# Gate and up products ahead of a data-dependent branch, in place of short products

## The chip, the cores and the metric

The kernel runs on one core of a Trainium2 chip. The metric is the device time of one execution in microseconds (us). TensorE (PE in the profile) multiplies, ScalarE (ACT), VectorE (DVE) and GpSimd (POOL) do the element work, SyncE (SP) issues the DMAs. PEld is TensorE's weight load, which overlaps its products.

## The reference

Four sequences of 1024 tokens, width 256, go through a half feed-forward step, an attention step with 16 heads, and a second half feed-forward step:

```python
x = x + 0.5 * ffn(_layernorm(x), gate_w, up_w, down_w, gate_s, up_s, down_s)
x = x + attn(_layernorm(x), Wq, Wk, Wv, Wo)          # causal, rotary, 16 heads of 16
x = x + 0.5 * ffn(_layernorm(x), gate_w, up_w, down_w, gate_s, up_s, down_s)

def ffn(xf, ...):
    g = jnp.einsum('th,ih->ti', xf, gate_w) * gate_s   # 704 hidden columns, weights -1, 0, 1
    u = jnp.einsum('th,ih->ti', xf, up_w) * up_s
    return jnp.einsum('ti,hi->th', jax.nn.silu(g) * u, down_w) * down_s
```

## The kernel before

Tokens go in chunks `c` of 512 (eight of them). The first feed-forward step works on one chunk at a time. DVE takes mean and variance of the rows (`dve_bn`, `dve_va`), POOL makes scale and shift of them (`pool_rs`, tile ROW, lines 1407 to 1412), ACT writes the normalized rows (`act_xn`, tile XN, line 1159, four operations a chunk), PE transposes them (`pe_xT`, line 996, eight products a chunk), and ACT and DVE split the result into a rounded part XH (`act_xh`, line 1165) and a rest XL (`dve_xl`, line 1267). [...]

A gate or up tile (`pe_g`, `pe_u`, line 1010) is one bank of PSUM, 128 hidden columns by 512 tokens. It takes four products of 128x512: XH and XL of the lower 128 inputs, then XH and XL of the upper 128. ACT takes silu of a gate tile (`act_silu`, tile G, line 1180), DVE multiplies it with the up tile (`dve_h`, tile HF, line 1301), ACT rounds that (`act_hh`, tile HH, line 1191), and POOL takes the rest (`pool_hl`, tile HL, line 1422, some 1.3 us each). There are two buffers of G and HF, so `dve_h` of a column block waits for `pool_hl` of the block two before it. The down projection (`pe_dn`, line 1039) reads HH and HL.

A planner (`timetable`) fixes the order on every engine before the program is built. Each engine runs its own list strictly in that order. The first PE entries are: short products on the identity IDT (`pe_warm`, line 988), the transposes of chunk 0, more short products, `pe_flag` (line 1017), one short product, `pe_branch`, then the tiles g0, g1, u0, u1, g2, u2, g3 of chunk 0, the transposes of chunk 1, the tiles g4, u3, u4, u5 of chunk 0 and g0, u0 of chunk 1, and the first half of the transposes of chunk 2. Gate tile i is written g(i), up tile i is u(i).

[...] DVE looks at the weights as they arrive (`dve_flag`, line 1273), `pe_flag` adds up over the partitions, DVE makes an integer of it (`dve_flagint`, lines 1280 and 1282, tile FLAG), and PE loads it into a register (line 1664) and branches (line 1666) into one of two copies of the rest of the program: float32r, or plain float32 where the flag is set. With the inputs of the reference the first copy runs. Between `pe_flag` and the register load stand eight short products of 128x128 in plain float32 (line 1661, `BEFORE_BRANCH = 8`), each run by the chip as two. PE goes into the branch with them queued.

The weights of gate and up come by DMA into RG and go from there by a second DMA into WG (`dma_wc0` to `dma_wc3`, line 1531). g0, g1 and u0 read columns of `dma_wc0`, u1 reads `dma_wc1`.

Of the kernel before, what the change touches and what calls it, by code (L numbers as in the profile page):

```python
# [17 lines left out]
P = 128  # L18
# [5 lines left out]
NI = 6  # L24
# [16 lines left out]
def gu_part(col):  # L41
    return next(i for i, (a, z) in enumerate(GU_COLS) if a <= col < z)
# [82 lines left out]
def e_skip(c2, j):  # L125
    return max(j - 4 * c2, 0) * P
# [202 lines left out]
BY_TANH = (0,)  # L329
AHEAD = 3.988  # L330
DOWN_FIRST = 4
BEFORE_BRANCH = 8
WARM_SPAN, WARM_SHARE, WARM_COLD = 2700.0, 0.5, 10000.0
BUSY = {"full": 0.92, "half": 0.85, "mask": 0.75, "col": 0.95}
FILL = {"full": "full", "half": "half", "mask": "half", "col": "half"}
# [86 lines left out]
def x_ring(who):  # L422
    return "X" + who
# [329 lines left out]
def macaron(nc, x_in, wgu, wd, wqkv, wo, gsc, usc, dsc, ident_in, cos_in, sin_in, mask_in, out):  # L753
    ctx = ExitStack()
    with ctx:
        cursor = [16512]

        def place(name, shape, dt=F32, at=None):
            size = int(np.prod(shape[1:])) * (2 if dt == BF16 else 4)
            off = cursor[0] if at is None else at  # L760
            t = nc.alloc_sbuf_tensor_at(name, list(shape), dt, offset=off)
            assert off + size <= 229344, (name, off + size)
            if at is None:
                cursor[0] = (off + size + 31) // 32 * 32
            return t

        def lay(at, *items):

            made = []
            for name, shape, dt in items:  # L770
                made.append(place(name, shape, dt, at=at))
                at += (int(np.prod(shape[1:])) * (2 if dt == BF16 else 4) + 31) // 32 * 32
            return made, at
# [4 lines left out]
        IDT = place("IDT", [P, P])  # L778
# [25 lines left out]
        XH = [place("XH0", [P, 2, 512], F32R)]  # L804
        XL = [place("XL0", [P, 2, 512], F32R)]
# [19 lines left out]
        OP, _ = lay(oc_at, *((f"{n}{i}", [P, 512], F32R) for i in range(4) for n in ("OL", "OH")))  # L825
# [40 lines left out]
        def f32(ap):  # L866
            return ap.bitcast(F32)
# [8 lines left out]
        def gu_slab(ph, kt, col):  # L876

            a, z = GU_COLS[gu_part(col)]
            at = 2 * a + kt * (z - a) + col - a
            return WG[ph][:, at:at + P]  # L880

        plan = timetable()
        slot, prior, emptied = plan.slot, plan.prior, plan.emptied
# [9 lines left out]
        pe, act, dve, pool, sp = (Engine(n, sems, done) for n in ("PE", "ACT", "DVE", "POOL", "SP"))  # L893
        S = sems | {signal: sems[sem] for signal, sem in EMPTIES.items() if sem in sems}

        def bank(*use):
            return psum[:, plan.bank[use][0], :]
# [5 lines left out]
        def x_slot(who, c):  # L903
            return {"a": (0,), "f1": (1, 2), "f2": (3, 0)}[who][slot[x_ring(who), (who, c)]]
# [37 lines left out]
        def wait_x_in(e, who, c, kt):  # L942
            e.wait_ge("act_xh", who, c, kt)
            e.wait_ge("dve_xl", who, c, kt)

        def wait_gu_weights(e, ph, col):
            if ph == 2:
                e.wait_ge("dma_w2")
            else:
                e.wait_ge(f"dma_wc{gu_part(col)}")  # L950
# [4 lines left out]
        def pt_view(gr, c2, j):  # L955

            s, off = pt_slot_of(c2, j)
            w = 512 - e_skip(c2, j)
            return PT[(PT_USES * gr + s) % PTN][:, 4 * off:4 * off + 4 * w].rearrange("p (h n) -> p h n", h=4)
# [4 lines left out]
                return f32(SH[gr % 2][:, 0, 0, :]).rearrange("p (a b t) -> p a b t", a=2, b=2)[:, :, :, t]  # L964
            return NP[gr % 2][:, ch, :].rearrange("p (a b t) -> p a b t", a=2, b=2)[:, :, :, t - 4]

        def tensor_program(e, todo, general):
            tn = nc.tensor

            def take(piece):  # L970

                for was in sorted(emptied.get(piece, ()), key=lambda was: -done[was]):
                    e.wait_ge(*was)
# [7 lines left out]
            for piece in todo:  # L981
                kind, a = piece[0], piece[1:]
# [6 lines left out]
                elif kind == "pe_xT":  # L989
                    who, c, kt = a  # L990
# [4 lines left out]
                    for i in range(4):  # L995
                        ins = tn.transpose(bank(*piece)[:, i * P:(i + 1) * P], XN[:, i, kt * P:(kt + 1) * P], IDT[:, :])  # L996
                    ins.then_inc(S["pe_xT"], 1)
                elif kind in ("pe_g", "pe_u"):
                    ph, c, i = a
                    who = f"f{ph}"  # L1000
                    k = x_slot(who, c)
                    col = 2 * P * i + (P if kind == "pe_u" and i < NI - 1 else 0)
                    wait_gu_weights(e, ph, col)
                    take(piece)
                    for kt in range(2):
                        wait_x_in(e, who, c, kt)
                        w = gu_slab(ph, kt, col)
                        for m, part in enumerate((XH, XL)):
                            x = part[k][:, kt, :]
                            ins = tn.matmul(bank(*piece), f32(w) if general else w, f32(x) if general else x,  # L1010
                                            start=(kt + m == 0), stop=(kt + m == 2))
# [6 lines left out]
                elif kind in ("pe_da", "pe_dn"):  # L1018
                    ph, c, pr, tt = a
# [17 lines left out]
                    for n, (part, i) in enumerate(terms):  # L1037
                        h, w = part[:, rows], WD[ph][:, i, :]
                        ins = tn.matmul(dst, f32(h) if general else h, f32(w) if general else w, start=(n == 0 and some[0] == 0),  # L1039
                                        stop=(n == len(terms) - 1 and some[-1] == NI - 1))  # L1040
                    ins.then_inc(S[kind], 1)
                elif kind == "pe_qk":
                    b, cc, w, ab = a
                    c = 2 * b + cc
                    k, cols = x_slot("a", c), slice((2 * w + ab) * P, (2 * w + ab + 1) * P)
# [6 lines left out]
                elif kind == "pe_v":  # L1052
                    b, cc, i = a
                    c = 2 * b + cc
                    k, rows = x_slot("a", c), slice(i * P, (i + 1) * P)
# [8 lines left out]
                elif kind == "pe_s":  # L1064
                    gr, t, ch, u = a
                    k, c2 = gr % QK, t // 4
# [6 lines left out]
                    for m, p in enumerate((0, 1) if u == "a" else (u,)):  # L1073
                        for hh in range(2):
                            dst = pair(*piece, hh)[:, p, :] if u == "a" else bank(*piece, hh)[:, 0:w]
                            r = slice(64 * hh, 64 * hh + 48)
                            ins = tn.matmul(dst, Q[k][r, p, t * P:(t + 1) * P], K[k][r, p, ch * 512:ch * 512 + w], start=(m == 0), stop=not diag)  # L1077
                    for half in range(2 if diag else 0):
                        for hh in range(2):
# [7 lines left out]
                            ins = tn.matmul(dst, EB[r, half, :], m, start=False, stop=(half == 1))  # L1087
                    ins.then_inc(S["pe_s"], 1)
                elif kind == "pe_st":
                    gr, c2, j, u = a  # L1090
                    k, skip = gr % QK, e_skip(c2, j)
# [6 lines left out]
                    for p in ((0, 1) if u == "a" else (u,)):  # L1098
                        for hh in range(2):
                            r = slice(64 * hh, 64 * hh + 50)  # L1100
                            dst = pair(*piece, hh)[:, p, :] if u == "a" else bank(*piece, hh)[:, base:512]
                            ins = tn.matmul(dst, K[k][r, p, j * P:(j + 1) * P], Q[k][r, p, 512 * c2 + base:512 * c2 + 512], start=True, stop=True)  # L1102
                    ins.then_inc(S["pe_st"], 1)
                elif kind == "pe_pv":
# [4 lines left out]
                    for j in (2 * jj, 2 * jj + 1):  # L1109
# [7 lines left out]
                        for h in (3, 2, 1, 0):  # L1117
                            col = VW * j + 17 * (4 * g + h)
                            ins = tn.matmul(bank(*piece)[32 * h:32 * h + 32, skip:512], V[b % 2][:, col:col + 32], pt_view(gr, c2, j)[:, h, :],  # L1119
                                            start=(j == 0), stop=(j == 4 * c2 + 3))  # L1120
# [16 lines left out]
        def scalar_program(e):  # L1137
            sc = nc.scalar
            for piece in plan.order["ACT"]:
# [42 lines left out]
                elif kind == "act_hh":  # L1182
                    ph, c, i = a
                    _, ul = h_lanes(i)
                    was = prior[f"hf{ph}", a]
                    e.wait_ge("dve_h", *a)
# [55 lines left out]
        def vector_program(e):  # L1242
            ve = nc.vector
            for piece in plan.order["DVE"]:
# [38 lines left out]
                elif kind == "dve_h":  # L1283
                    ph, c, i = a
                    _, ul = h_lanes(i)
                    k = slot[f"Gf{ph}", a]
                    was = prior[f"Gf{ph}", a]
# [15 lines left out]
                elif kind == "dve_hl":  # L1303
                    ph, c, i = a
                    _, ul = h_lanes(i)
                    s = slot[f"hf{ph}", a]
                    e.wait_ge("act_hh", *a)
# [325 lines left out]
        @block.sync  # L1633
        def _(eng):
            sp.eng = eng
            sync_program(sp)
# [16 lines left out]
        @block.tensor  # L1653
        def _(eng):
            pe.eng = eng
            todo = plan.order["PE"]
            cut = todo.index(("pe_branch",))
            tensor_program(pe, todo[:cut], True)
            held = next(piece for piece in reversed(todo[:cut]) if piece[0] == "pe_warm")
            for _ in range(BEFORE_BRANCH):  # L1660
                nc.tensor.matmul(bank(*held)[:, 0:P], IDT[:, :], IDT[:, :], start=True, stop=True)
            pe.wait_ge("dve_flagint")
            flag = nc.tensor.alloc_register("general")
            nc.tensor.reg_load(flag, FLAG[0:1, 0:1])
            before = dict(pe.met)
            with nc.tensor.If_eq(flag, 0):
                tensor_program(pe, todo[cut + 1:], False)
            pe.met = before
            with nc.tensor.Else():
                tensor_program(pe, todo[cut + 1:], True)  # L1670


def rope_tables():
# [59 lines left out]
```

## Time and profile before

| | us |
|---|---|
| median of 3 runs | 796.4 |
| lowest, highest run | 794.45, 797.7 |
| the profiled execution, whole | 796.11 |
| its span, first to last instruction | 794.1 |
| PE busy | 772.8 |
| ACT, DVE, POOL busy | 549.4, 614.1, 390.1 |

The profile is of one execution. Times in the rows are from the span's start. Whole time less span is 2.0 us, and the median is 0.3 us above the profiled execution.

### The profile page before, as it was taken

The numbers are of one execution on the slowest core, as the hardware profiler recorded it, in microseconds if no ns is written. First come the engines' busy times: TensorE is split into PE (matmuls) and PEld (weight loads), VectorE is DVE, ScalarE is ACT, GpSimd is POOL, SyncE is SP. The second block draws the span as 40 slices with busy tenths as digits, with TensorE's granted clock in tenths as the row PEclk, the third lists the DMA queues.
The fourth block names the chain that finished last, engine by engine and source line by source line (L and its number), as shares of the span: only waits on it lengthen the run. The fifth ranks groups of instructions, "written<-read, shape, count | busy, mean of one in ns | idle before, by whom it ended". The sixth has DMA issues, their size and how long they took to land.

```text
span 794.1 us, 17285 instructions
## 1 busy us (share of the span) xinstructions
PE 772.8 (97%) x6160; PEld 524.9 (66%) x6160; DVE 614.1 (77%) x1267; ACT 549.4 (69%) x1064; POOL 390.1 (49%) x430
## 2 busy tenths in 40 slices
PE   6999999999999999999999999999999999999997
PEld 6888888777555555665554566555555457898886
DVE  5767577799898997997998799989988925465543
ACT  3866675445867878767787867778877997466652
POOL 3887777536425643153282143531322256566554
PEclk9999999999999999999999999999999999999999
DMA  8801263204364585254573453643741210210001
GB/s 329 350 3 57 103 159 118 45 3 93 112 177 141 173 223 142 60 123 140 170 194 130 115 125 124 174 102 82 222 109 55 64 44 19 67 37 28 27 27 55
DMA packets 61089, 89.76 MB, mean 113 GB/s; under 512 B 19788, under 2 KB 24268, under 8 KB 60748
## 3 DMA queue, kind: packets, MB, share of 16 engines
q1 hardware_dynamic: 60860, 88.57, 38.7%
q8 instruction: 52, 0.85, 0.5%
q14 instruction: 33, 0.27, 0.1%
q10 hardware_dynamic: 144, 0.07, 0.0%
HBM read 45.52 MB, written 40.76 MB: 109 GB/s over the span
## 4 chain that ended last, share of the span: by engine, by line
PE 83%; DVE 9%; ACT 3%; issue 2%; POOL 2%; DMA 1%; SPq 0%; DVEq 0%; ACTq 0%
PE psum L1010 17%; PE psum L1119 15%; PE psum L978 12%; PE psum L1102 12%; PE psum L1039 11%; PE psum L1077 10%; DVE NP L1362 4%; PE psum L1087 3%; DVE SH L1362 2%; PE psum L996 2%; ACT PT L1227 1%; POOL HL_f L1422 1%; DMA RD<-wd 1%; PE psum L988 1%; DVE HF_f L1301 1%
## 5 line engine op out<-in xcount | busy, mean ns | idle before, releaser
L1227 ACT ACTIVATE PT<-psum 128x512 f32<-128x512 f32 (+2 forms) x640 | 309.8, 572 | 99.2 <-PE psum L1102 97.7
L1362 DVE TENSOR_REDUCE NP<-psum 128x1 f32<-128x512 f32 (+3 forms) x448 | 261.1, 643 | 21.8 <-PE psum L1087 14.1
L1479 POOL TENSOR_SCALAR_AFFINE_SELECT PT<-PT 128x512 f32<-128x512 f32 x128 | 80.5, 635 | 182.7 <-ACT PT L1227 182.5
L1119 PE MATMUL psum<-PT,V 128*32 128x512 f32 (+3 forms) x1536 | 143.8, 492 | 0.0
L1102 PE MATMUL psum<-Q,K 50*128 50x512 f32 (+2 forms) x768 | 141.7, 408 | 1.8 <-DVE XL L1267 0.7
L1077 PE MATMUL psum<-K,Q 48*128 48x512 f32 (+2 forms) x768 | 138.3, 386 | 5.0 <-ACT PT L1227 2.6
L1010 PE MATMUL psum<-XH,WG_f 128*128 128x512 f32 x352 | 141.6, 402 | 0.1
L1010 PE MATMUL psum<-XL,WG_f 128*128 128x512 f32 x352 | 138.3, 393 | 0.0
L1422 POOL TENSOR_TENSOR HL_f<-HF_f,HH_f 128x512 fp32r<-128x512 f32 x80 | 103.1, 1298 | 70.3 <-ACT HH_f L1191 70.1
L1362 DVE TENSOR_REDUCE SH<-psum 128x1 f32<-128x512 f32 (+3 forms) x192 | 103.4, 591 | 13.4 <-PE psum L1087 12.6
L1102 PEld LDWEIGHTS psum<-Q,K 50*128 50x128 f32 x768 | 67.3, 185 | 70.0 <-DVE NP L1362 24.4
L1301 DVE SCALAR_TENSOR_TENSOR HF_f<-psum,US,G_f 128x512 f32<-128x512 f32 x90 | 67.3, 750 | 56.1 <-ACT G_f L1180 31.3
L1180 ACT ACTIVATE G_f<-psum,GS 128x512 f32<-128x512 f32 x90 | 61.4, 684 | 58.5 <-PE psum L1010 58.0
L1077 PEld LDWEIGHTS psum<-K,Q 48*128 48x128 f32 x768 | 71.9, 185 | 37.8 <-DVE NP L1362 15.1
L1039 PE MATMUL psum<-WD_f,HH_f 128*128 128x256 f32 x384 | 88.9, 286 | 1.9 <-DVE HH_f L1308 1.1
L1191 ACT ACTIVATE HH_f<-HF_f 128x512 fp32r<-128x512 f32 x96 | 60.4, 631 | 34.1 <-DVE HF_f L1301 33.2
L1119 PEld LDWEIGHTS psum<-PT,V 128*32 128x32 f32 x1536 | 40.1, 109 | 64.7 <-issue 47.4
L1039 PE MATMUL psum<-WD_f,HL_f 128*128 128x256 f32 x320 | 79.2, 283 | 0.0
L1010 PEld LDWEIGHTS psum<-XH,WG_f 128*128 128x128 f32 x352 | 66.2, 188 | 17.4 <-issue 2.3
L1010 PEld LDWEIGHTS psum<-XL,WG_f 128*128 128x128 f32 x352 | 66.3, 188 | 12.9
L1039 PEld LDWEIGHTS psum<-WD_f,HH_f 128*128 128x128 f32 x384 | 69.9, 190 | 5.0 <-issue 2.4
L1039 PEld LDWEIGHTS psum<-WD_f,HL_f 128*128 128x128 f32 x320 | 60.8, 190 | 0.2
(88 smaller groups left out, 1050.9 us busy)
## 6 DMA issues: line engine op xcount, KB each, us to landing
zd<-ZH SPq DMA_DIRECT2D x32, 512.0 KB, 3.8
Q<-zd SPq DMA_DIRECT2D x64, 192.0 KB, 3.7
K<-zd SPq DMA_DIRECT2D x64, 192.0 KB, 4.7
zd<-ZL SPq DMA_DIRECT2D x16, 512.0 KB, 4.6
od<-OS SPq DMA_DIRECT2D x32, 256.0 KB, 2.3
OC<-od SPq DMA_DIRECT2D x32, 128.0 KB, 2.7
SC<-rd_ SPq DMA_DIRECT2D x32, 128.0 KB, 2.9
X<-x SPq DMA_DIRECT2D x7, 512.0 KB, 11.9
```

The source lines that it names most:

```text
L978: ins = tn.matmul(dst, x, w, start=(m == 0), stop=(m == len(terms) - 1))
L1010: ins = tn.matmul(bank(*piece), f32(w) if general else w, f32(x) if general else x, start=(kt + m == 0), stop=(kt + m == 2))
L1039: ins = tn.matmul(dst, f32(h) if general else h, f32(w) if general else w, start=(n == 0 and some[0] == 0), stop=(n == len(terms) - 1 and ...
L1077: ins = tn.matmul(dst, Q[k][r, p, t * P:(t + 1) * P], K[k][r, p, ch * 512:ch * 512 + w], start=(m == 0), stop=not diag)
L1102: ins = tn.matmul(dst, K[k][r, p, j * P:(j + 1) * P], Q[k][r, p, 512 * c2 + base:512 * c2 + 512], start=True, stop=True)
L1119: ins = tn.matmul(bank(*piece)[32 * h:32 * h + 32, skip:512], V[b % 2][:, col:col + 32], pt_view(gr, c2, j)[:, h, :], start=(j == 0), stop ...
L1180: sc.activation(G[ph][slot[f"Gf{ph}", a]][gl if turned else ul, :], bank(*gate)[gl, :], ACT.Tanh if turned else ACT.Silu, scale=(GSH if tu ...
L1227: sc.activation(dst, src, ACT.Exp, scale=0.25).then_inc(S["act_exp"], 1)
L1301: ve.scalar_tensor_tensor(HF[ph][k][ul, :], bank("pe_u", *a)[ul, :], (UG if turned else US)[ul, i:i + 1], G[ph][k][ul, :], ALU.mult, ALU.m ...
L1362: ve.tensor_reduce(out=acc, in_=src, axis=AX, op=ALU.max, negate=True).then_inc(S["dve_max"], 1)
L1422: gp_.tensor_tensor(HL[ph][s][:, :], HF[ph][slot[f"Gf{ph}", a]][:, :], f32(HH[ph][s][:, :]), ALU.subtract).then_inc(S["pool_hl"], 1)
L1479: gp_.affine_select(out=pt, in_=pt, compare_op=ALU.is_ge, fill=0.0, base=0, pattern=[[0, 4], [1, P]], channel_multiplier=-1).then_inc(S["p ...
```

## The change

The eight short products in front of the register load go. In their place stand three of the four products of the first four tiles behind the branch (g0, g1, u0, u1): XH and XL of the lower half of the inputs with the first weight slab, XH of the upper half with the second. They are in float32r in any case. Behind the branch the float32r copy gives each of the four tiles its fourth product (XL of the upper half). The plain copy starts the four tiles afresh, with all four products.

```diff
-BEFORE_BRANCH = 8
+BEFORE_BRANCH = 4
...
+        def begin_tiles(e, tiles):
+
+            for piece in tiles:
+                kind, ph, c, i = piece
+                k, col = x_slot("f1", c), gate_or_up(kind, i)
+                wait_gu_weights(e, ph, col)
+                assert ph == 1 and not emptied.get(piece)
+                e.wait_ge("act_xh", "f1", c, 0)
+                nc.tensor.matmul(bank(*piece), gu_slab(ph, 0, col), XH[k][:, 0, :], start=True, stop=False)
+                e.wait_ge("act_xh", "f1", c, 1)
+                nc.tensor.matmul(bank(*piece), gu_slab(ph, 1, col), XH[k][:, 1, :], start=False, stop=False)
+                e.wait_ge("dve_xl", "f1", c, 0)
+                nc.tensor.matmul(bank(*piece), gu_slab(ph, 0, col), XL[k][:, 0, :], start=False, stop=False)
...
-                    take(piece)
+                    if piece not in begun:
+                        take(piece)
                     for kt in range(2):
                         wait_x_in(e, who, c, kt)
+                    if piece in begun:
+                        ins = tn.matmul(bank(*piece), gu_slab(ph, 1, col), XL[k][:, 1, :], start=False, stop=True)
+                    for kt in range(2 if general or piece not in begun else 0):
...
-            held = next(piece for piece in reversed(todo[:cut]) if piece[0] == "pe_warm")
-            for _ in range(BEFORE_BRANCH):
-                nc.tensor.matmul(bank(*held)[:, 0:P], IDT[:, :], IDT[:, :], start=True, stop=True)
+            begun = todo[cut + 1:cut + 1 + BEFORE_BRANCH]
+            begin_tiles(pe, begun)
             pe.wait_ge("dve_flagint")
```

The list of PE around the branch, before. `waits` names the semaphores that an instruction waits for:

```order
L1017 MATMUL psum<-FL,CST 1x6 [waits pool_const,dve_flags]
L988 MATMUL psum<-IDT 128x128
L1661 MATMUL psum<-IDT 128x128 x8
L1664 TENSOR_LOAD FLAG [waits dve_flagint]
L1666 COMPARE_AND_BRANCH
L1010 MATMUL psum<-XH_143,WG_f_119 128x512 [waits dve_out,act_out,dma_wc0]
L1010 MATMUL psum<-XL_144,WG_f_119 128x512
```

The same place of the changed kernel. Lines 978, 980 and 982 are the three products, line 1026 is the fourth, line 1031 the line 1010 of before:

```order
L1038 MATMUL psum<-FL,CST 1x6 [waits pool_const,dve_flags]
L1005 MATMUL psum<-IDT 128x128
L978 MATMUL psum<-XH_143,WG_f_119 128x512 [waits act_out,dma_wc0]
L980 MATMUL psum<-XH_143,WG_f_119 128x512 [waits act_out]
L982 MATMUL psum<-XL_144,WG_f_119 128x512 [waits dve_out]
...
L978 MATMUL psum<-XH_143,WG_f_119 128x512 [waits dma_wc1]
L980 MATMUL psum<-XH_143,WG_f_119 128x512
L982 MATMUL psum<-XL_144,WG_f_119 128x512
L1684 TENSOR_LOAD FLAG [waits dve_flagint]
L1686 COMPARE_AND_BRANCH
L1026 MATMUL psum<-XL_144,WG_f_119 128x512 [waits dve_out]
L1026 MATMUL psum<-XL_144,WG_f_119 128x512 x3
```

Twelve long products and the waits for `dma_wc0` and `dma_wc1` stand in front of the register load now. The list of ACT behind its first two roundings is the same in both kernels but for the line numbers; here it is of before:

```order
L1180 ACTIVATE G_f_121<-psum,GS 128x512 [waits pe_g]
L1159 ACTIVATE XN<-X,ROW 128x256 [waits pool_rs]
L1180 ACTIVATE G_f_122<-psum,GS 128x512 [waits pe_g]
L1159 ACTIVATE XN<-X,ROW 128x256 x3
L1191 ACTIVATE HH_f_127<-HF_f_123 128x512 [waits dve_out]
L1191 ACTIVATE HH_f_129<-HF_f_124 128x512 [waits dve_out]
```

No entry of ACT, DVE, POOL or SP has moved.

## Rows read from the trace of the kernel before

**Rows 1.** The page, part 1: busy time, share of the span, instructions.

```profile
PE 772.8 (97%) x6160; PEld 524.9 (66%) x6160; DVE 614.1 (77%) x1267; ACT 549.4 (69%) x1064; POOL 390.1 (49%) x430
```

**Rows 2.** The chain that ended last, 13 to 31 us: start, length, what.

```profile
16.54 1.17 PE psum L1010 x4
17.73 0.69 ACT G_f L1180
...
19.48 1.47 ACT XN L1159 x3
20.96 0.53 ACT HH_f L1191
...
21.56 2.53 POOL HL_f L1422 x2
...
26.00 1.26 POOL HL_f L1422
...
27.38 0.76 DVE HF_f L1301
...
29.53 0.61 ACT XN L1159
```

**Rows 3.** The timeline of PE: start, length, what, count, idle time before and its releaser.

```profile
14.02 0.19 PE L1017 MATMUL psum<-FL,CST 128*1 128x6 f32 x2 [1.28 <-DVE FL L1277]
...
14.47 1.95 PE L1661 MATMUL psum<-IDT 128*128 128x128 f32 x16
16.54 0.47 PE L1010 MATMUL psum<-XH,WG_f 128*128 128x512 f32 x1
16.84 0.40 PE L1010 MATMUL psum<-XL,WG_f 128*128 128x512 f32 x1
...
17.30 0.39 PE L1010 MATMUL psum<-XL,WG_f 128*128 128x512 f32 x1
...
19.34 0.39 PE L1010 MATMUL psum<-XH,WG_f 128*128 128x512 f32 x1
...
22.98 1.04 PE L996 MATMUL psum<-IDT,XN 128*128 128x128 f32 x8
...
30.28 0.63 PE L996 MATMUL psum<-IDT,XN 128*128 128x128 f32 x4 [0.81 <-ACT XN L1159]
...
788.95 0.28 PE L1039 MATMUL psum<-WD_f,HH_f 128*128 128x256 f32 x1
```

**Rows 4.** The timeline of PEld, 14.8 to 16.6 us.

```profile
14.69 1.53 PEld L1661 LDWEIGHTS psum<-IDT 128*128 128x128 f32 x13
16.50 0.19 PEld L1010 LDWEIGHTS psum<-XH,WG_f 128*128 128x128 f32 x1 [0.28 <-issue]
```

**Rows 5.** The register load in the view of tile FLAG.

```profile
L1664 PEldq TENSOR_LOAD <-FLAG x1: 1334/1334/1334, 14.9 to 14.9; - x1
```

**Rows 6.** The timeline of DVE around the flag.

```profile
13.21 0.68 DVE L1267 TENSOR_TENSOR XL<-psum,XH 128x512 fp32r<-128x512 f32 x1
...
14.70 0.14 DVE L1282 CAST FLAG<-CST 1x1 int32<-1x1 f32 x1
```

**Rows 7.** Line 1531, all four issues, `dma_wc0` first, with time to landing.

```profile
L1531 SPq DMA_DIRECT2D WG_f<-RG x4: 465/530/686, 7.2 to 10.4; - x4
...
DMA to landing us min/median/max: 7.0/7.1/7.2
```

**Rows 8.** Line 1531, the issue of `dma_wc1` alone.

```profile
L1531 SPq DMA_DIRECT2D WG_f<-RG x1: 483/483/483, 8.3 to 8.3; - x1
```

**Rows 9.** The timeline of POOL: the last scale row of chunk 1.

```profile
17.72 0.20 POOL L1412 TENSOR_TENSOR ROW<-ROW 128x4 f32<-128x4 f32 x1
```

**Rows 10.** PE by stretch: length, busy time, count, granted clock, DMA share, GB/s.

```profile
4.20:7.90 3.70, 3.67 (x17) 1.00 0.87 282
791.00:793.00 2.00, 0.00 (x0) 1.00 0.25 72
```

More of the change, by code:

```diff
@@ L965, in maxima_of, with gate_or_up, tensor_program @@
             return NP[gr % 2][:, ch, :].rearrange("p (a b t) -> p a b t", a=2, b=2)[:, :, :, t - 4]
-        def tensor_program(e, todo, general):
+        def gate_or_up(kind, i):
+            return 2 * P * i + P * (kind == "pe_u" and i < NI - 1)
+        def begin_tiles(e, tiles):
[10 more added lines that the diff above has]
+                nc.tensor.matmul(bank(*piece), gu_slab(ph, 0, col), XL[k][:, 0, :], start=False, stop=False)
+        def tensor_program(e, todo, general, begun=()):
             tn = nc.tensor
@@ L1001, in tensor_program @@
                     k = x_slot(who, c)
-                    col = 2 * P * i + (P if kind == "pe_u" and i < NI - 1 else 0)
+                    col = gate_or_up(kind, i)
                     wait_gu_weights(e, ph, col)
-                    take(piece)
+                    if piece not in begun:
+                        take(piece)
                     for kt in range(2):
                         wait_x_in(e, who, c, kt)
+                    if piece in begun:
+                        ins = tn.matmul(bank(*piece), gu_slab(ph, 1, col), XL[k][:, 1, :], start=False, stop=True)
+                    for kt in range(2 if general or piece not in begun else 0):
                         w = gu_slab(ph, kt, col)
@@ L1666, in _ @@
             with nc.tensor.If_eq(flag, 0):
-                tensor_program(pe, todo[cut + 1:], False)
+                tensor_program(pe, todo[cut + 1:], False, begun)
             pe.met = before
             with nc.tensor.Else():
-                tensor_program(pe, todo[cut + 1:], True)
+                tensor_program(pe, todo[cut + 1:], True, begun)
 def rope_tables():
```

## The prediction

> **What bounds the kernel now.** The page first: PE is busy for 97% of the span [rows 1], so the first guess is that 2 us of dummy work in front of the branch, replaced by useful products, is 2 us off the end. Whether it is has to be read from the stretch itself, and the view for that is the chain that ended last, from 13 to 31 us [rows 2]. What to see there: the chain is on PE for the four products of g0, the first gate tile, from 16.54 us, and leaves PE at 17.71. It goes over ACT (silu of g0, then the rows XN of chunk 1 and a second silu without a break to 20.96, then the first HH), POOL (two HL, the scale rows of chunk 2, a third HL from 26.00), DVE (HF at 27.38) and ACT (XN at 29.53), and comes back to PE at 30.28, for the transposes of chunk 2. PE's own timeline shows the same from the other side: it has no idle time from 16.54 on until it stands for 0.81 us for this XN [rows 3]. So between 17.7 and 30.28 us PE is full but not the bound. Whatever is won on PE there only lengthens that wait, unless silu of g0 starts earlier.
>
> **What the branch costs now.** The integer flag is written at 14.70 + 0.14 = 14.84 us [rows 6], the register load starts at 14.9 and takes 1.33 [rows 5], and the first weight load of g0 follows at 16.50 [rows 4]: 1.66 us from flag to first work behind the branch. The 16 short products run meanwhile, 14.47 to 16.42 [rows 3], and hide all but 0.12 us of it.
>
> **The change, step by step.** All of it is in the first 20 us. Three times decide when g0 is complete.
>
> Start of the new products. They wait for XH and XL of chunk 0 (long there: even the upper half of XL is written by 13.21 + 0.68 = 13.89 [rows 6]), and for `dma_wc0`: issue 7.2, landing 7.1 later, 14.3 to 14.4 us [rows 7]. PE comes free of the last short product in front of them where the removed ones began, at 14.47 [rows 3]. The two meet, and I take 14.47 as the start.
>
> Time of the twelve. The first step behind short products is 16.84 - 16.54 = 0.30 us, the later ones are (19.34 - 17.30) / 9 = 0.227 [rows 3]. The thirteenth product, which is the fourth of g0, can start at 14.47 + 0.30 + 11 x 0.227 = 17.27 us.
>
> Branch. The register load now stands behind the wait for `dma_wc1`: 8.3 + 7.1 = 15.4 us [rows 7, 8], 0.6 us after the flag. That the load doesn't also wait for the queued products to run shows in its start at 14.9, when 11 or so of the 16 short weight loads (13 from 14.69 on, over 1.53 us) were still to come [rows 4, 5]; twelve long products are no longer a queue than those 16. How fast PE's sequencer gets through its list: from `pe_flag` at 14.02 to the load at 14.9 it passed 2 + 2 + 16 products and as many weight loads [rows 3, 5], 0.9 us for 40, at most 22 ns each. Three products and their loads stand behind the last wait: 0.13 us. So the register load starts at about 15.5 and work behind the branch is possible from 15.5 + 1.6 = 17.1 to 17.2 us. That is before 17.27: the branch stays hidden, by 0.1 us. This is the thinnest cover in the change; each 0.1 us more of landing or dispatch beyond it delays g0 by as much.
>
> The Trainium skill, "TensorE: Matmul & The Clock Gate", section "Step-by-step: what each phase is for", says that the sequencer may spend about 62 ns on each MATMUL where hardware decode is off. Were that so for loads and products alike, the 24 instructions behind the landing of `dma_wc0` would take 1.5 us and the fourth product of g0 would come some 0.3 us late; the 40 instructions in 0.9 us don't agree with it.
>
> Sum for g0. Its fourth product started at 17.30 [rows 3] and will start at 17.27. Silu of g0 started at 17.73 [rows 2] and will at 17.70: 0.03 us gained.
>
> What the 2.07 us on PE turn into. Thirteen products are done where one was begun, so everything in PE's list behind them can be 19.34 - 17.27 = 2.07 us earlier. u0 is complete 1.4 us earlier and the first HF with it, but HH of it stands behind the XN of chunk 1 in ACT's list, which end at 20.96 as before [rows 2]. So POOL's first HL stays at 21.56, with it the two HL, the scale rows, the third HL, the HF that waits for that one for want of a third buffer, and the last XN. The transposes of chunk 1 have 22.98 - 2.07 = 20.91 us as PE's own time; their XN end at 20.96, so they start at about 21.0 and pass on nearly all of the lead. Six more tiles follow, for which banks are free by then: silu and HF, which free them, are no later than before. PE then stands before the transposes of chunk 2 not for 0.81 but for about 0.81 + 2.0 = 2.8 us. They start at 30.28 - 0.03. From there on nothing in the lists differs.
>
> Even a much earlier g0 would bring little: silu of g0 is followed on ACT by the first XN of chunk 1, and the scale row for that ends at 17.72 + 0.20 = 17.92 [rows 9], while ACT is busy with the silu to 17.73 + 0.69 = 18.42 [rows 2]. So no more than 0.5 us could come that way.
>
> **Sum.** 794.1 - 0.03 for the span, 2.0 around it: 796.1 us for the profiled execution, and 0.3 more for the median of the runs: 796.4 us. For the unknown parts: both landings now have almost no slack where they had 2 us and more, and the latest of three nearly equal times decides. If they scatter by some tenths, g0 is on average 0.1 to 0.3 us later. I leave this inside the range, since it is below what shows.
>
> **Rivals.**
>
> The lead gets through. If the chain from silu of g0 to 30.28 isn't what holds XN of chunk 2 (for instance if the earlier HF let HH and HL move up), up to 2.07 us arrive: 796.4 - 2.1 = 794.3 us. For it speaks PE's 97% [rows 1]. Against it, every link from 19.48 to 29.53 follows the one before without a gap worth naming, and none is PE [rows 2].
>
> The branch is no longer covered. If the register load has to wait until the products in front of it have been taken by the array, it starts at about 16.9 (the twelfth weight load) in place of 15.5, work behind it starts at 18.5, and g0 is 1.2 us late, which the chain passes on in full: 797.6 us. It decides from the point at which the load starts later than 15.6. Against it stands the load at 14.9 with weight loads still queued [rows 4, 5].
>
> The clock falls. PE's idle stretch grows from 0.81 to 2.8 us, the longest since its first product. The record gives a granted clock of 1.00 (2.4 GHz) in all of this, and also at 791 to 793 us, when the last product had ended at 788.95 + 0.28 = 789.23 [rows 3, 10]: 3.8 us idle with the clock still up. If it falls all the same, PE restarts at 30.28 slowly, and from there the chain is on PE. The price by the slowest stretch in the rows, whatever its recorded clock: 17 short products in 3.70 us at the start, 0.22 each, against 16 in 1.95, 0.12 each [rows 3, 10], so in 3.7 us some 1.7 to 1.9 us are lost: 798.3 us. It decides from an idle time at which the clock has dropped, which is more than 2.8 us by the end of this trace.
>
> The same page of the Trainium skill, section "HAM oscillation — how this bites in real kernels", warns of this: idle gaps that are long enough throttle the array to 1.2 GHz. Here the 1.28 us gap before 14.02 [rows 3] didn't.
>
> **Chances and range.** No change beyond 0.3 us: 0.82. Lead gets through, in part or whole: 0.07. Branch uncovered: 0.05. Clock falls: 0.04. Something else: 0.02. Predicted: 796.4 us, by the first case. The runs of before themselves spread from 794.45 to 797.7, so that case alone needs about 794.5 to 797.9; the range takes in the rivals to 794.3 and 798.3. A measurement of this kernel can tell about 0.5%, 4 us, from no change. None of the cases reaches that, so faster 0.01, same 0.97, slower 0.02.
>
> **What would show it.** Right: the new products start at 14.5 and step by 0.23; the register load starts at 15.4 to 15.6; there is no idle time of PE around 17.2; silu of g0 starts at 17.7; the transposes of chunk 1 start at 21.0; PE waits 2.8 us for XN and goes on at 30.2 to 30.3. PE's count falls by 16 to 6144 and its busy time by about 2. Wrong: a silu of g0 past 18 (landing or branch), transposes of chunk 2 before 29.5 (the chain was another), or products after 30.3 at twice the step (clock).

## The result, and the profile after

The changed kernel took 797.11 us, median of 22 executions (793.92 to 798.23), against 795.65 for the kernel before on the same chips (22 executions). The ratio is 1.0018, 95% interval 1.0010 to 1.0026: slower by a hair, but clear of its interval. The predicted 796.4 us lies 0.7 us off and the time is inside the range. That flatters the prediction: its 796.4 us stood on three runs of before, and 22 of them have 795.65. It forecast no change, and the change was 1.5 us. That nothing would change was wrong.

The traced execution of the changed kernel took 793.92 us, and it was the fastest of the 22, with a span of 791.9 us. So the trace of it can't show what made the others slower; it does show every step of the prediction. Page, part 1 (answers to [rows 1]), 16 products fewer:

```profile
PE 771.5 (97%) x6144; PEld 522.8 (66%) x6144; DVE 614.0 (78%) x1267; ACT 549.4 (69%) x1064; POOL 390.2 (49%) x430
```

The timeline of PE, changed kernel (answers to [rows 3]):

```profile
13.64 0.19 PE L1038 MATMUL psum<-FL,CST 128*1 128x6 f32 x2 [0.95 <-DVE FL L1298]
...
14.01 0.48 PE L978 MATMUL psum<-XH,WG_f 128*128 128x512 f32 x1
14.33 0.39 PE L980 MATMUL psum<-XH,WG_f 128*128 128x512 f32 x1
...
16.62 0.39 PE L982 MATMUL psum<-XL,WG_f 128*128 128x512 f32 x1
16.84 1.20 PE L1026 MATMUL psum<-XL,WG_f 128*128 128x512 f32 x4
...
20.75 1.06 PE L1013 MATMUL psum<-IDT,XN 128*128 128x128 f32 x8
...
29.93 0.63 PE L1013 MATMUL psum<-IDT,XN 128*128 128x128 f32 x4 [2.65 <-ACT XN L1180]
```

The twelve new products run from 14.01 us without a break into the four behind the branch (16.62, then 16.84). The transposes of chunk 1 are 2.2 us earlier than in [rows 3], and PE then stands 2.65 us where it stood 0.81. In the chain (answers to [rows 2]) the same links follow each other, all 0.35 us earlier because the flag was that much earlier in this execution:

```profile
17.37 0.69 ACT G_f L1201
...
20.60 0.53 ACT HH_f L1212
...
21.20 2.55 POOL HL_f L1443 x2
...
29.19 0.61 ACT XN L1180
29.80 0.14 issue
29.93 0.63 PE psum L1013 x4
```

So the lead of 2 us is there and is lost whole in front of the transposes of chunk 2. What made the kernel slower stands in the list of executions instead. Each has a mean granted clock, and the changed kernel's were:

| mean granted clock | executions of 22 | their times, us |
|---|---|---|
| 0.996 or 0.997 | 10 | 796.69 to 798.05 |
| 0.998 | 4 | 797.15 to 798.23 |
| 0.999 or 1.000 | 8 | 793.92 to 796.81 |

The traced one had 1.000.

### The profile page after: what moved, and what is told of

The parts are those of the page before. It is cut to its first block, busy times and chain, and to the rows that moved or that the text cites. A ratio compares the mean times of both kernels' runs of the same rounds, so it can differ in the third digit from the quotient of the medians.

```text
span 791.9 us, 17254 instructions
## 1 busy us (share of the span) xinstructions
PE 771.5 (97%) x6144; PEld 522.8 (66%) x6144; DVE 614.0 (78%) x1267; ACT 549.4 (69%) x1064; POOL 390.2 (49%) x430
## 4 chain that ended last, share of the span: by engine, by line
PE 83%; DVE 9%; ACT 3%; issue 2%; POOL 2%; DMA 1%; SPq 0%; DVEq 0%; ACTq 0%
PE psum L1031 17%; PE psum L1140 15%; PE psum L995 12%; PE psum L1123 12%; PE psum L1060 11%; PE psum L1098 10%; DVE NP L1383 4%; PE psum L1108 3%; DVE SH L1383 2%; PE psum L1013 2%; ACT PT L1248 1%; POOL HL_f L1443 1%; DMA RD<-wd 1%; PE psum L1005 1%; ACT XN L1180 1%
## 5 line engine op out<-in xcount | busy, mean ns | idle before, releaser
L1031 PE MATMUL psum<-XH,WG_f 128*128 128x512 f32 x344 | 138.3, 402 | 0.0
L1031 PE MATMUL psum<-XL,WG_f 128*128 128x512 f32 x344 | 135.0, 393 | 0.0
L1212 ACT ACTIVATE HH_f<-HF_f 128x512 fp32r<-128x512 f32 x96 | 60.4, 631 | 34.1 <-DVE HF_f L1322 33.2
L1031 PEld LDWEIGHTS psum<-XH,WG_f 128*128 128x128 f32 x344 | 64.6, 188 | 17.0 <-issue 2.0
L1031 PEld LDWEIGHTS psum<-XL,WG_f 128*128 128x128 f32 x344 | 64.7, 188 | 12.7
```

## The experiments

**The changed kernel again.** No edit.

> The changed kernel as it is, for the granted clock of each execution and a second trace. Clock theory: the executions whose mean granted clock is 0.998 or less take some 797 to 798 us, those at 0.999 or 1.000 some 796, and if the traced one is of the former, its clock stands at 1.2 GHz for some us right behind PE's wait before 29.9 us. Branch theory (the branch is uncovered in many executions): the time doesn't go with the clock, and silu of g0 starts after 18 us in the traced one. Ratio to before 1.001 to 1.003 by both.

Measured: 796.05 us median of 12, ratio 1.0002 (0.9989 to 1.0015), so the median alone shows no change this time. The four executions at 0.997 or less took 797.47 to 799.37 us, those at 1.000 took 793.97 to 796.16. Four of the five at 0.998 took only 795.29 to 795.51 us, not the 797 to 798 expected; more on these below. The traced execution was at 0.997. PE by stretch (length, busy, granted clock, DMA share, GB/s):

```profile
27.60:29.80 2.20, 0.01 (x1) 1.00 1.04 413
29.80:33.20 3.40, 2.95 (x9) 0.50 0.94 359
33.20:36.00 2.80, 2.80 (x22) 1.00 0.96 402
```

The timelines of PE and of ACT (silu of g0) in the same execution:

```profile
17.04 0.40 PE L982 MATMUL psum<-XL,WG_f 128*128 128x512 f32 x1
17.27 1.09 PE L1026 MATMUL psum<-XL,WG_f 128*128 128x512 f32 x4
...
30.25 1.09 PE L1013 MATMUL psum<-IDT,XN 128*128 128x128 f32 x4 [2.64 <-ACT XN L1180]
```

```profile
17.71 0.69 ACT L1201 ACTIVATE G_f<-psum,GS 128x512 f32<-128x512 f32 x1 [4.16 <-PE psum L1026]
```

The wait is 2.64 us, as long as in the first trace, but here the granted clock goes to 0.50 (1.2 GHz) at 29.80 us and comes back at 33.2. The first transposes take 1.09 us where they took 0.63. Up to the wait the execution is on time to 0.02 us: fourth product of g0 at 17.27, silu at 17.71. In this execution the branch isn't it. The next transposes start 1.37 us later than in the trace of before, the down products behind them 1.07 us later, before first and this execution second:

```profile
32.58 0.60 PE L996 MATMUL psum<-IDT,XN 128*128 128x128 f32 x4
33.24 0.36 PE L1039 MATMUL psum<-WD_f,HH_f 128*128 128x256 f32 x1
```

```profile
33.95 0.60 PE L1013 MATMUL psum<-IDT,XN 128*128 128x128 f32 x4
34.31 0.36 PE L1060 MATMUL psum<-WD_f,HH_f 128*128 128x256 f32 x1
```

So 0.3 us of the loss went into a wait that PE has before the down products in any case. The other 1.07 us are still 1.00 us at the end. The fall cost 1.0 to 1.1 us, although PE came out of its wait 0.03 us earlier than before did.

**The kernel before again.** No edit.

> The kernel before as it is, for the granted clock of each execution. Clock theory: nearly all executions have a mean granted clock of 0.999 or 1.000, since the wait before 30.3 us is 0.8 us long. If before shows 0.996 to 0.998 as often as the changed kernel does, the clock theory falls. Ratio 0.999 to 1.001.

Measured: 795.77 us median of 11, ratio 0.9991 (0.9982 to 1.0000). No execution at 0.997 or less, three at 0.998. The three pools of the kernel before that ran beside the experiments had 35, 35 and 29 executions, and none of these was below 0.998 either. A mean of 0.998 alone says little, since the clock also goes to 0.5 behind the last product and how much of the span's end that covers differs between executions. The ratio is one of a kernel against itself, so a pair of medians can stand 0.09% apart without any change.

**The changed kernel, its wait filled.** In front of the wait for XN of chunk 2, in both copies of the program:

```diff
                     e.wait_ge("act_id")
+                    take(piece)
+                    for _ in range(9 if piece[1:] == ("f1", 2, 0) else 0):
+                        tn.matmul(bank(*piece)[:, 0:P], IDT[:, :], IDT[:, :], start=True, stop=True)
                     for i in range(4):
                         e.wait_ge("act_xn", who, c, i)
-                    take(piece)
```

> The changed kernel with nine short products on the identity (some 2.0 us) put in front of PE's wait for the rows XN of chunk 2, so that PE stands for 0.6 us and not for 2.65. Clock theory: no execution below 0.999, and the time comes back to that of before, ratio 0.999 to 1.001. Branch theory or landing theory: the fill changes nothing, ratio 1.001 to 1.003.

Measured: 795.91 us median of 11, ratio 0.9996 (0.9986 to 1.0007). One execution at 0.996 (797.97 us), not none as expected, two at 0.998. PE's timeline:

```profile
27.50 2.17 PE L1011 MATMUL psum<-IDT 128*128 128x128 f32 x18
...
30.29 0.63 PE L1015 MATMUL psum<-IDT,XN 128*128 128x128 f32 x4 [0.62 <-ACT XN L1182]
```

With dummy work in the lead's place the ratio is that of before. By the medians alone that isn't told from the changed kernel beside it (1.0002); by the clocks it is 1 of 11 against 4 of 12, and 1 of 23 against 15 of 45 with the half-filled wait and the third measurement below. The one low execution wasn't traced, so where its clock fell is open. Two more took 797.16 and 797.92 us at 0.998, while of 110 executions of before only four took more than 797. What slowed these three is open too.

**The kernel before, with a wait as long.** The branch and its short products stay; nine products of 128x512 between the branch and the wait are left out, so a part of the computation is missing:

```diff
+                    thin = ph == 1 and (c == 0 and piece[0:1] + a[2:] not in (("pe_g", 0), ("pe_g", 1), ("pe_u", 0), ("pe_u", 1)) or c == 1 and i == 0)
...
+                            if thin and (kt, m) == (0, 1):
+                                continue
```

> The kernel before, its branch and short products untouched, with the lower XL product left out of nine tiles between the branch and the transposes of chunk 2 (g2, u2, g3, g4, u3, u4, u5 of chunk 0, g0 and u0 of chunk 1); this part of the computation is missing. PE's wait before 30.3 us grows by 9 x 0.227 = 2.0 us to 2.8. Clock theory: as in the changed kernel, about half or more of the executions at 0.996 to 0.998, ratio 1.001 to 1.003 although there is less work. Branch theory: ratio 0.999 to 1.001.

Measured: 796.22 us median of 11, ratio 1.0001 (0.9990 to 1.0012): below the 1.001 to 1.003 expected of the clock theory, and within what the branch theory allowed. The clocks tell more than the median: four of 11 at 0.997 or less, at 797.14 to 798.70 us, and the traced one among them:

```profile
30.25 0.63 PE L996 MATMUL psum<-IDT,XN 128*128 128x128 f32 x4 [2.82 <-ACT XN L1162]
```

```profile
28.00:31.60 3.60, 1.35 (x8) 1.00 0.96 370
31.60:35.05 3.45, 3.45 (x13) 0.51 1.03 404
35.05:50.00 14.95, 14.95 (x90) 1.00 0.16 63
```

Here the wait is 2.82 us, and the clock only falls 1.4 us after PE is back at work. PE ends 1.15 us later than in the trace of before. Four more executions are at 0.998, so 8 of 11 are at 0.998 or less, the half or more that was expected. Less work, same branch as before, and the fall is there: it comes with the wait.

**The kernel before, with a longer wait.** The condition above takes in a second product, so twice as much of the computation is missing:

```diff
-                            if thin and (kt, m) == (0, 1):
+                            if thin and (kt, m) in ((0, 1), (1, 0)):
```

> The kernel before with both the lower XL and the upper XH product left out of the same nine tiles (part of the computation is missing). PE's wait before the transposes of chunk 2 grows to 0.8 + 18 x 0.227 = 4.9 us. Clock theory: now every execution loses the clock there, so all are at 0.998 or less and most at 0.997 or less, and the median is some 1.3 us above that of before. If the share of such executions stays at that of the 2.8 us wait (4 of 11), the length of the wait isn't what decides.

Measured: 797.66 us median of 12, ratio 1.0026 (1.0016 to 1.0037). That is 2.0 us above the kernel before beside it (795.69), for 1.3 expected. Eleven of 12 at 0.997 or less, the twelfth at 0.998. PE's wait was 4.16 us (4.9 expected; where the rest went wasn't looked at), the clock was low for twice as long, and PE ended 1.64 us later than in the trace of before:

```profile
26.00:27.80 1.80, 0.09 (x1) 1.00 1.04 414
27.90:34.60 6.70, 4.36 (x13) 0.50 0.89 352
34.70:40.00 5.30, 5.30 (x47) 1.00 0.59 241
```

**The changed kernel, its wait half filled.** Four short products in place of the nine.

> The changed kernel with four short products (0.9 us) in front of the same wait, so that it is some 1.7 us long. Clock theory with the length of the wait deciding: fewer executions at 0.997 or less than the changed kernel has (14 of 34), at most 2 of 11, ratio 0.999 to 1.001. A theory on which any break beyond 1 us is enough: as many as in the changed kernel.

Measured: 795.69 us median of 12, ratio 0.9997 (0.9986 to 1.0008). The wait was 1.75 us and no execution was at 0.997 or less, where at most 2 of 11 were expected.

Put together, with the length of the longest wait behind the branch as the traces have it:

| kernel | PE's longest wait behind the branch, us | executions at 0.997 or less |
|---|---|---|
| changed, filled | 0.7 | 1 of 11 |
| nine entries moved (below) | 0.85 | 1 of 12 |
| before, its own and three pools | 0.8 and 0.9 | 0 of 110 |
| four entries moved, two measurements (below) | 1.63 | 0 of 24 |
| changed, half filled | 1.75 | 0 of 12 |
| changed, three tiles (below) | 2.45 | 2 of 12 |
| changed, three measurements | 2.65 | 15 of 45 |
| before, one product less | 2.82 | 4 of 11 |
| before, two products less | 4.16 | 11 of 12 |

Up to 1.75 us that is 2 of 169, from 2.45 us on 32 of 80. The count misses falls. 3.4 us at half the clock take 0.002 off the mean of 794 us, which gives 0.998; to reach 0.997 the clock must also be low for some 0.6 us at the span's end. Before has 21 executions at 0.998, none below 795.72 us. The changed kernel has five at 795.21 to 795.51 us, the one with a product less three at 795.04 to 795.10. They are most likely falls in executions that ended early, but none of them was traced. So take the table for the trend, and its shares as lower bounds.

**Three tiles ahead of the branch.**

```diff
-BEFORE_BRANCH = 4
+BEFORE_BRANCH = 3
```

> Only the first three tiles (g0, g1, u0: nine products) begin ahead of the branch. By the working of the prediction the ninth product starts at 16.6 us and the branch, which no longer stands behind the second weight landing, is ready at 16.5: still covered. g0 then ends 0.6 to 0.7 us earlier than in the changed kernel, and the scale rows of chunk 1 on POOL let 0.3 to 0.5 us of it through: PE is back for the transposes of chunk 2 some 0.3 us earlier after the flag than in the changed kernel. PE's wait is 2.3 us. Clock theory: executions at 0.997 or less are somewhat fewer than 14 of 34. Rival, branch not covered by nine: a break of PE of 0.3 us or more before the first product behind the branch.

Measured: 795.76 us median of 12, ratio 1.0002 (0.9992 to 1.0011); two at 0.997 or less. PE, ACT and the register load:

```profile
16.25 0.40 PE L982 MATMUL psum<-XL,WG_f 128*128 128x512 f32 x1
16.48 0.91 PE L1026 MATMUL psum<-XL,WG_f 128*128 128x512 f32 x3
```

```profile
16.96 0.69 ACT L1201 ACTIVATE G_f<-psum,GS 128x512 f32<-128x512 f32 x1 [3.55 <-PE psum L1026]
17.83 0.60 ACT L1180 ACTIVATE XN<-X,ROW 128x256 f32<-128x256 f32 x1 [0.18 <-POOL ROW L1433]
```

```profile
L1684 PEldq TENSOR_LOAD <-FLAG x1: 1432/1432/1432, 14.8 to 14.8; - x1
```

Nine products do cover the branch, silu of g0 starts 0.75 us earlier than in the second trace of the changed kernel, and the next operation of ACT now waits for POOL's scale row: the 0.5 us that the prediction allowed for that way were 0.45, since the transposes of chunk 2 started at 29.80 against 30.25. It is a gain too small to show in the ratio.

**The changed kernel a third time.** No edit.

> The changed kernel once more, for more executions. Clock theory: again about 4 or 5 of 12 with a mean granted clock of 0.997 or less, and those about 1.3 us above the others; ratio 1.000 to 1.002. If none falls, the share differs between chips and the theory's size is open.

Measured: 796.57 us median of 11, ratio 1.0009 (1.0000 to 1.0018). One execution at 0.997 or less, fewer than expected, and five at 0.998, four of them at 796.85 to 797.14 us. Over the three measurements the changed kernel has 45 executions with a mean of 796.6 us and before has 110 with 795.7: 0.9 us or 0.11%. One by one, each against before beside it, the means differ by 1.4, 0.4 and 0.35 us, and the executions at 0.997 or less were 10 of 22, 4 of 12 and 1 of 11. That it is slower stands; by how much is uncertain. The 15 at 0.997 or less have a median of 797.5, the 16 at 0.999 or more 796.1, those of before at 0.999 or more 795.9.

**Work in the way of the lead.** On top of the three tiles, four entries of the planner's lists are moved:

```diff
+    put("PE", ("pe_g", 1, 1, 1), ("pe_xT", "f1", 2, 0))
+    put("PE", ("pe_u", 1, 1, 1), ("pe_xT", "f1", 2, 0))
+    put("ACT", ("act_hh", 1, 0, 5), ("act_wh", "q"))
+    put("POOL", ("pool_wl", "o"), ("pool_hl", 1, 2, 0))
```

`put` takes an entry out of an engine's list and puts it ahead of another.

> As the kernel with three tiles, and four entries of the lists moved so that PE's lead meets work and not a wait: g1 and u1 of chunk 1 in front of the transposes of chunk 2 on PE, the last HH of chunk 0 in front of the rounding of the q, k, v weights on ACT, the rest of the output weights on POOL behind the scale rows of chunk 4 (where POOL had 2.3 us idle). Chain theory (ACT and POOL hold the start, PE follows): the wait before 30 us shrinks to 0.4 us or less, the down products of chunk 0 start 1.3 to 1.8 us earlier, POOL's chain is 1.3 us shorter, and PE ends 1 to 1.6 us earlier than in before; no execution at 0.997 or less; ratio 0.998 to 0.999. If PE is what holds the start, the moves change nothing beyond the 0.3 us of the three tiles: ratio 0.9995 to 1.0005.

Measured: 795.32 us median of 12, ratio 0.9995 (0.9984 to 1.0006), none at 0.997 or less. PE:

```profile
29.85 1.06 PE L1023 MATMUL psum<-IDT,XN 128*128 128x128 f32 x8 [0.68 <-ACT XN L1190]
31.61 0.36 PE L1070 MATMUL psum<-WD_f,HH_f 128*128 128x256 f32 x1 [0.69 <-DVE HH_f L1339]
...
49.65 0.36 PE L1070 MATMUL psum<-WD_f,HH_f 128*128 128x256 f32 x1 [1.63 <-DVE HH_f L1339]
```

At 45 us PE was 1.6 us ahead of the trace of before, at 55 us 0.6: a second wait, for the last HH of chunk 1, took 1 us back. The 1 to 1.6 us expected at the end came as 0.65 (last product at 788.30 against 788.95).

> The kernel with three tiles and four moved entries once more. PE's waits are 0.7, 0.7 and 1.6 us long there, so by the clock theory none of 12 at 0.997 or less; ratio 0.9990 to 1.0000.

The repetition: 795.46 us median of 12, ratio 0.9999 (0.9990 to 1.0008), none at 0.997 or less. PE ends 0.4 us earlier than in the trace of before. No measurable gain.

**Five more entries.** On top of that:

```diff
+    put("POOL", ("pool_hl", 1, 1, 1), ("pool_x", 1, 0, 0))
+    put("DVE", ("dve_t2", 1, 0, 1), ("dve_bn", "f1", 4, 0))
+    put("DVE", ("dve_h", 1, 1, 2), ("dve_bn", "f1", 4, 1))
+    put("DVE", ("dve_h", 1, 1, 3), ("dve_bn", "a", 0, 1))
+    put("DVE", ("dve_hl", 1, 1, 5), ("dve_h", 1, 2, 0))
```

> As moved, and five more entries moved, so that its 1.6 us lead at 45 us isn't given back at 49.65 us, where PE waits 1.63 us for the rest of the last HH of chunk 1 (DVE does it behind an HF that waits for PE itself): that rest now stands ahead of that HF, POOL takes the second HL of chunk 1 ahead of the two updates of X, and DVE the HF of blocks 2 and 3 of chunk 1 ahead of statistics. If the order of DVE and POOL is what gives the lead back, the down products of chunk 1 start at 48.0 to 48.5 us and PE ends 1.5 to 2 us earlier than in before, ratio 0.997 to 0.999. If a later wait takes it (the one at 72 us), PE ends 0.6 to 1 us earlier as in moved, ratio 0.999 to 1.000.

Measured: 794.58 us median of 12, ratio 0.9981 (0.9970 to 0.9992). It is the only change with an interval clear of 1 on the fast side, and the interval also lies below that of the changed kernel beside it (1.0000 to 1.0018). It was measured once. PE:

```profile
29.45 1.06 PE L1028 MATMUL psum<-IDT,XN 128*128 128x128 f32 x8 [0.46 <-ACT XN L1195]
31.21 0.36 PE L1075 MATMUL psum<-WD_f,HH_f 128*128 128x256 f32 x1 [0.69 <-DVE HH_f L1344]
48.47 0.36 PE L1075 MATMUL psum<-WD_f,HH_f 128*128 128x256 f32 x1 [0.85 <-DVE HH_f L1344]
```

The wait of 1.63 us is now 0.85. PE is 2.0 us ahead of the trace of before at 45 us, 1.8 at 55 and 1.9 at the end. Half a microsecond of this is the flag, which was that much earlier in this execution (its sum at 13.52 against 14.02 us in [rows 3]); the other 1.4 are the lead, carried to the end. One untraced execution of the 12 was at 0.997 or less (796.11 us).

## Why the prediction was wrong, point by point

**The start, right.** 14.47 us was taken for the first new product, from the landing of `dma_wc0`. It came at 14.01 in the first trace, in which the flag was also 0.4 us early, and the twelve took 16.84 - 14.01 = 2.83 us (predicted 2.80). In the second trace the fourth product of g0 started at 17.27 and silu of g0 at 17.71, against 17.27 and 17.70. The scatter of the landings that the prediction allowed for shows once: with the wait half filled the first new product came 0.68 us behind the start of `pe_flag`, in the other four traces with twelve products ahead 0.36 to 0.49.

**The branch, covered as said, its price not constant.** The register load does wait for the second weight landing and not for the queued products: in the second trace it started at 15.4, for a landing at 15.35. What I took as fixed is not: the load itself took 1.33 us in the trace of before. In others:

```profile
L1684 PEldq TENSOR_LOAD <-FLAG x1: 1668/1668/1668, 15.0 to 15.0; - x1
```

```profile
L1684 PEldq TENSOR_LOAD <-FLAG x1: 1461/1461/1461, 15.4 to 15.4; - x1
```

```profile
L1664 PEldq TENSOR_LOAD <-FLAG x1: 732/732/732, 14.6 to 14.6; - x1
```

These are the changed kernel twice, and the kernel before again. Where it is short, the kernel before profits. In the last of these the first product of g0 came 1.70 us behind the first short one (14.08), in [rows 3] 2.07 us behind it (14.47):

```profile
15.78 0.48 PE L1010 MATMUL psum<-XH,WG_f 128*128 128x512 f32 x1
```

So the branch cost before some 0.37 us in [rows 3], and not the 0.12 that the prediction read off the modelled end of the last short product. The sum doesn't use that number. Silu of g0 started at 16.99 us there and not at 17.73; 0.39 of this is an earlier flag, the rest the shorter load. The changed kernel can't profit, since its g0 stands behind twelve products whatever the branch does. But the load also took 1.57 us in one trace with the branch of before, and there g0 came 0.2 us later behind `pe_flag`. From the start of `pe_flag` to silu of g0 the four traces with the branch of before took 3.36 to 3.95 us, 3.70 on average, the five with twelve products 3.62 to 3.96, 3.75 on average. So the branch and the landings account for some 0.05 us. The executions at 0.999 or more differ by 0.2 us in their medians (796.1 and 795.9).

**Where the lead goes, right.** The chain of silu, XN, HH, HL, HF and XN again held the transposes of chunk 2 in every trace of the changed kernel, and PE's wait grew to 2.65 us (predicted 2.8). The rival in which the lead gets through would have given 794.3 us and didn't come, until the lists were changed for it.

**The clock, where the prediction failed.** The mechanism was named as a rival, at its place, with 0.04. By the clocks it came in at least 15 of 45 executions. The step that failed is the bound on it: from one idle stretch at the end of one trace (3.8 us with the granted clock at 1.00, [rows 3, 10]) I concluded that 2.8 us are safe. Three traces of the same kernel have the same wait, 2.65, 2.64 and 2.64 us, and only the second has the fall. So the length of the wait alone doesn't decide, and one idle stretch that passed doesn't make a shorter one safe. The ends of the traces say the same: PE was idle for 3.8 us before the clock fell in the trace of before, but for 2.4 us in the first trace with four entries moved (last product done at 788.59, granted clock 0.50 from 790.95) and for over 4 in the first of the changed kernel. What else decides is open; over many executions the share grows from 2 of 169 up to 1.75 us to 11 of 12 at 4.16. The step is wrong in kind, not in size. The price was mis-sized as well: 1.1 us measured for a wait of 2.64 us, for 1.7 to 1.9 predicted, because in the 3.4 us at 1.2 GHz PE had 2.95 us of work, not 3.7, and half of that is 1.5 us; 0.3 of it went into the wait before the down products. The rule of the Trainium skill that the prediction quoted and held the 1.28 us wait against ("TensorE: Matmul & The Clock Gate", "HAM oscillation — how this bites in real kernels") agrees in kind: behind long waits the clock stood at 1.2 GHz. The section gives an idle time as the limit, and the fall at 2.64 us came below it, so here the measurement decides.

How far this fills the 0.9 us between the means is an estimate. The 15 executions at 0.997 or less, at 1.1 us each, make 0.4 us of it. (They lie 1.9 us above the mean of before, but most that are at 0.997 also ended late, so 1.9 is not the price of a fall.) If the 14 at 0.998 are nearly all falls too, it is 0.7 us. In their favour: 24 of 45 executions of the changed kernel took 796.8 us or more, of before 5 of 110. The rest of 0.2 to 0.5 us isn't traced to anything.

**The size of 0.18%.** It is somewhat large, for a reason that has nothing to do with the change. The last of the output writes lands 1.7 to 1.8 us after its issue, or 2 us later: in the view of the output tensor the last two writes of before took up to 3.5 us, those of the changed kernel 1.8.

```profile
DMA to landing us min/median/max: 1.7/2.6/3.5
```

```profile
DMA to landing us min/median/max: 1.7/1.8/1.8
```

Both kernels have both cases. In the first measurement 8 of 22 executions of before and 1 of 22 of the changed kernel were below 795 us, in the others the changed kernel had 3 more of 23. Counting the five at 0.998 below 795.6 us as early ones that lost 1.1 us to a fall, the changed kernel has 9 of 45, before 23 of 110. Then the cases are as frequent in both, and the 1 of 22 was luck. Between kernels that are 1 to 2 us apart such a pair of cases weighs as much as the change.

The prediction gave "no change" its high chance also because a measurement was taken to tell no less than 0.5%. With 22 executions on either side the interval was 0.16% wide.

## What to carry to other kernels

Work that is brought forward on an engine which the chain doesn't pass through only lengthens that engine's next wait. Ask before the change what stands at that wait, and move what feeds it as well: alone the change cost 0.1%; with nine entries of the lists moved and one tile less ahead of the branch the kernel was 0.2% faster than before, in one measurement of 12 executions. On TensorE a longer wait isn't free: one execution's trace, with or without a fall of the clock, doesn't tell how often it falls, so read the granted clock of many executions, and fill a wait of 2 us or more with dummy products if nothing else is at hand.

## What was not expected of the hardware

The granted clock went to 0.50 for 3.4 us in two traces, and for 6.8 us with a wait of 4.16, also while PE was busy: in one the fall came 1.4 us after the wait had ended. A load of one word into a register of TensorE's sequencer took from 0.73 to 1.67 us in the traces of one kernel and its variants. The very last write landed 1.7 to 1.9 us after its issue in five of the 13 traces and 3.5 to 4.0 us in the other eight, with nothing between. One execution of 11 with the wait filled and one of 12 with the nine moved entries had a clock of 0.997 or less although the traces of their kernels show no wait of PE beyond 1 us behind the branch; why is open.
